# Sending k's rounded parts ahead of q's, and negating the row maxima ahead of k's roundings

## What is computed

```
xn = layernorm(x)
q, k, v = xn Wq + bq, xn Wk + bk, xn Wv + bv      # 32 query heads, 8 key/value heads, width 64
q, k = rope(q) * SCALE, rope(k) * SCALE            # interleaved pairs: first and second component
scores = q . k, masked to |i - j| <= 128, with one sink logit per head
s = softmax([scores, sink])[..., :-1] v, projected by Wo, + bo
g = silu(fp8_quantised(xn) W_ffn + b_ffn)
out = x + s * g
```

## Time and profile before

| what | value |
|---|---|
| runs | 1755.33 us median of 3 (1750.91 to 1756.24) |
| the profiled execution | 1750.54 us, span 1748.8 us |
| mean granted TensorE clock | 0.966 |
| PE busy | 1636.6 us (94% of the span) |
| DVE busy | 1170.5 us (67%) |
| POOL busy | 1024.7 us (59%) |
| ACT busy | 992.4 us (57%) |
| PE waiting at L1126, put down to "issue" | 23.5 us in 8 waits, longest 3.3 us |

### The profile page before, as it was taken

The page is one execution under the profiler, slowest core; times in us unless marked ns, Lnnn a source line. Parts: engine busy times, 40 slices in busy tenths (PEclk is TensorE's granted clock), DMA queues, the critical chain, the costliest instruction groups (busy, mean ns, idle before and its releaser), DMA issues.

```text
span 1748.8 us, 33908 instructions
## 1 busy us (share of the span) xinstructions
PE 1636.6 (94%) x11139; PEld 1466.8 (84%) x11139; DVE 1170.5 (67%) x3643; ACT 992.4 (57%) x2405; POOL 1024.7 (59%) x1019
## 2 busy tenths in 40 slices
PE   3289999999999999999999999999999999999998
PEld 2168998989979898899979999898988999799987
DVE  7766666666767667576666666666775767676664
ACT  2245665666655665556655666556665566555663
POOL 3445656576556656566665755656574676566651
PEclk9579999999999999999999999999999999999999
DMA  4534542535344543454434344355434444434540
GB/s 163 138 64 82 103 79 61 110 70 97 70 86 90 98 91 63 86 94 91 89 69 94 76 95 82 67 103 99 84 61 100 82 94 84 77 69 86 104 82 13
DMA packets 79678, 150.88 MB, mean 86 GB/s; under 512 B 12688, under 2 KB 28816, under 8 KB 75408
## 3 DMA queue, kind: packets, MB, share of 16 engines
q1 hardware_dynamic: 79504, 148.71, 42.6%
HBM read 18.64 MB, written 4.19 MB: 13 GB/s over the span
## 4 chain that ended last, share of the span: by engine, by line
PE 88%; issue 3%; DVE 3%; ACT 1%; POOL 0%; DMA 0%; SPq 0%; POOLq 0%; DVEq 0%
PE pv_bank L1165 29%; PE ring L1071 12%; PE ring L1126 11%; PE acc L1190 10%; PE score L1149 8%; PE score L1151 8%; PE ring L1175 4%; PE ring L1080 3%; PE ring L1102 1%; PE ring L1061 1%; DVE junk L878 1%; DVE ffn_e L773 0%; PE ring L1041 0%; DMA x_in<-in_x 0%; DVE k_first_hi L856 0%
## 5 line engine op out<-in xcount | busy, mean ns | idle before, releaser
L878 DVE CUSTOM_DVE_ANT_0 junk<-ring,mask,sink 128x384 bf16<-128x384 f32 (+1 forms) x1024 | 559.5, 549 | 325.8 <-PE ring L1126 309.3
L1165 PEld LDWEIGHTS pv_bank<-v,stage 128*128 128x128 f32 x5120 | 687.6, 192 | 32.6 <-ACT stage L608 11.1
L1165 PE MATMUL pv_bank<-v,stage 128*128 128x65 f32 x5120 | 688.6, 266 | 4.1 <-DVE o_norm L893 3.2
L528 POOL TENSOR_SCALAR_AFFINE_SELECT stage<-stage 128x512 f32<-128x512 f32 x384 | 251.5, 667 | 506.7 <-ACT stage L608 506.0
L608 ACT ACTIVATE stage<-score 128x512 f32<-128x512 f32 x640 | 372.9, 597 | 217.7 <-PE score L1151 209.0
L1126 PE MATMUL ring<-kT_high,qT_full 128*128 128x384 f32 (+1 forms) x1024 | 372.7, 364 | 46.8 <-issue 23.5
L1149 PE MATMUL score<-qT_full,kT_high 128*128 128x512 f32 x640 | 266.1, 416 | 0.0
L1126 PEld LDWEIGHTS ring<-kT_high,qT_full 128*128 128x128 f32 x1024 | 197.2, 193 | 81.5 <-issue 36.5
L1151 PE MATMUL score<-qT_high,kT_low 68*128 68x512 f32 x640 | 256.0, 400 | 0.0
L666 ACT ACTIVATE oT_hi<-ring 128x256 fp32r<-128x256 f32 x256 | 96.8, 378 | 181.8 <-PE ring L1175 179.9
L643 ACT ACTIVATE qT_high<-ring,ident 4x256 fp32r<-4x256 f32 x512 | 196.0, 451 | 4.7 <-PE ring L1102 1.7
(11 more groups left out here) (114 smaller groups left out, 2605.1 us busy)
## 6 DMA issues: line engine op xcount, KB each, us to landing
qT_high<-qT_full SPq DMA_DIRECT2D x64, 512.0 KB, 4.5
qT_full<-q_first SPq DMA_DIRECT2D x64, 256.0 KB, 4.2
qT_full<-q_first_hi SPq DMA_DIRECT2D x64, 256.0 KB, 5.3
qT_full<-q_second SPq DMA_DIRECT2D x64, 256.0 KB, 4.1
qT_full<-q_second_hi SPq DMA_DIRECT2D x64, 256.0 KB, 5.3
kT_high<-k_first_hi SPq DMA_DIRECT2D x128, 64.0 KB, 2.5
kT_high<-k_second_hi SPq DMA_DIRECT2D x128, 64.0 KB, 2.4
x_res<-in_x SPq DMA_DIRECT2D x11, 512.0 KB, 6.1
```

Source lines behind the costliest of these rows:

```text
L528: nc.gpsimd.affine_select(out=pr, in_=pr, compare_op=ALU.is_ge, fill=0.0, base=0, pattern=[[0, GROUP], [sign, P]], channel_multiplier=-sign) \
L878: nc.vector.tensor_tensor_reduce(junk[:, h % 2, 0:cols], ring[h % 2][:, 0:cols], mask[:, m0:m0 + cols], 1.0, sink[:, col:col + 1], ALU.add ...
L1165: last = nc.tensor.matmul(pv[:, h, :], prob[:, q % 2 * 3 + n, h * P:(h + 1) * P], v[:, slot, k, :], start=(n == 0), stop=(n == len(BLOCKS[ ...
```

## The change

On SP `keys_in` is split. The four transfers of the rounded parts (`keys_high_in`) wait for k's roundings (`s_k_hi`) alone, the two of the low parts (`keys_low_in`) for the subtractions (`s_k_lo`), as before. At k = 6 the four stand in front of the first component of q, and the two stay where all six were. On ACT `negated` moves in front of `keys_first_high`, `chunk_high`, `ffn_exp` and `scale_x`, and `keys_second_high` goes right behind `keys_first_high`.

```
-            def keys_in(t):
+            def keys_high_in(t):
                 quad, r = t // QUAD, slice(t % QUAD, P, QUAD)
-                sp.wait_ge(s_k_lo, 2 * quad + 2)
+                sp.wait_ge(s_k_hi, 2 * quad + 2)
                 upto(sp, s_score_pe, NB * (t - 2))
                 upto(sp, s_kT_in, K_IN * t)
                 for row, part in ((0, k_first_hi), (HALF, k_second_hi), (D, k_first_hi), (D + HALF, k_second_hi)):
                     sp.dma_start(kT_high[row:row + HALF, t % 3, :].bitcast(F32), part[r, :]).then_inc(s_kT_in, 16)
+
+            def keys_low_in(t):
+
+                quad, r = t // QUAD, slice(t % QUAD, P, QUAD)
+                sp.wait_ge(s_k_lo, 2 * quad + 2)
                 for row, part in ((0, k_first), (HALF, k_second)):
                     sp.dma_start(kT_low[row:row + HALF, t % 3, :].bitcast(F32), part[r, :]).then_inc(s_kT_in, 16)
...
                 if real(t) and t % QUAD:
-                    keys_in(t)
+                    keys_high_in(t)
+                    keys_low_in(t)
                 if real(t) and k == 2:
-                    keys_in(t)
+                    keys_high_in(t)
+                    keys_low_in(t)
+                if real(t) and k == 6:
+                    keys_high_in(t)
                 if real(a):
                     queries_in(a, False)
                 if real(t) and k == 6:
-                    keys_in(t)
+                    keys_low_in(t)
                 if real(a):
                     queries_in(a, True)
...
                     if q == 2 and real(a):
                         first_high(a)
+                    if q == 0 and real(it):
+                        negated(it, 1)
+                    if q == 2 and real(b):
+                        negated(b, 0)
                     if (k, q) in ((2, 0), (6, 2)) and quad < BATCH * QUADS:
                         keys_first_high(quad)
+                        keys_second_high(quad)
                     if it < 0 and fill + FIRST_CHUNKS < N_CHUNKS:
                         chunk_high(fill + FIRST_CHUNKS)
                     if (k, q) in ((2, 2), (4, 2)) and 0 <= n < BATCH:
                         ffn_exp(n, k // 2 - 1)
                     if (k, q) == (6, 0) and 1 <= n + 1 < BATCH:
                         scale_x(n + 1)
-                    if q == 0 and real(it):
-                        negated(it, 1)
-                    if q == 2 and real(b):
-                        negated(b, 0)
-                    if (k, q) in ((2, 0), (6, 2)) and quad < BATCH * QUADS:
-                        keys_second_high(quad)
```

## The result

| | before | changed |
|---|---|---|
| median of 4 runs | 1753.12 us (1745.76 to 1756.24) | 1729.70 us (1726.83 to 1737.31) |
| the profiled execution | 1750.54 us | 1731.17 us |
| span | 1748.8 us | 1729.4 us |
| mean granted clock | 0.966 | 0.973 |

The ratio is 0.9882, 95% interval 0.9849 to 0.9916: 1.2% faster. The forecast was 1730.0 us, 25.3 us less than a median of 1755.33; a fourth execution of the kernel before, 1745.76 us, has brought that median down to 1753.12. The medians differ by 23.4 us, the two profiled executions by 19.4 us. What follows explains the 19.4, since the traces are of these.

A forecast was written before the change was run, and what follows sets the result against it. PE, busy for 94%, bounds the kernel, with waits for q's second component at k = 6. 14.9 (queue) + 12.2 (clock) + 2.4 (start-up) - 4.2 (k = 2) = 25.3 us, from 1755.3 to 1730.0 us; range 1722 to 1746.

The forecast's parts named there:

- SP's queue at k = 6: At k = 6, q's second component goes out earlier, so PE restarts 2.13 us earlier a batch, 14.9 us over seven.
- POOL 0.39 us later at k = 6 through `scale_x`: In slot 0 of k = 6, `scale_x` behind `negated` makes the exponentials 0.67 us later; 0.39 us of it remain on POOL.
- PE's arrival: At k = 6, PE was taken to reach its wait at 288.92 as before, leaving a wait of 0.94 us.
- The clock: Behind the waits at k = 6, the shorter wait no longer brings the clock down: 12.2 us, bounds nothing to 14.5.
- k = 2: At k = 2, ACT's roundings behind `negated` delay `max_rows` and PE by 0.53 us, eight times: 4.2 us lost.
- Rival 1: At k = 6, the shorter wait still brings the clock down: 1742 us, chance 0.22.
- The start-up: At the start, q's second component goes out earlier and PE's 9.1 us wait shrinks by 2.4 us, bounds 1 to 2.4.
- Rival 2: At k = 6, q's second component lands later behind its first: only 0.7 us a batch won, about 1752 us, chance 0.05.
- The sum: Over the whole kernel, all terms together gain 25.3 us: profiled execution 1725.2 us, median 1730.0 us.

The follow-up runs named there:

- e1: SP's part of the change alone, ACT's order as in the kernel before: 1713.29 us, ratio 0.9804.
- e2: ACT's part of the change alone, on the kernel before, SP's order as before: 1759.39 us, ratio 1.0060.
- e6: The full change, but with `scale_x` in front of `negated` again in slot 0 of k = 6: 1718.55 us, ratio 0.9823.
- e7: The full change, but with k's first rounding in front of `negated` again in slot 0 of k = 2: 1725.22 us, ratio 0.9853.
- e4: The full change, with k's low parts behind `second_low` on POOL and behind q's second component on SP at k = 6: 1722.44 us, ratio 0.9853.
- e3: SP's part, and of ACT's part only `negated` in front of k's roundings in slot 2: 1716.37 us, ratio 0.9820.
- e5: SP's part alone, with k's low parts last on POOL and SP at k = 6 as in e4: 1710.31 us, ratio 0.9774.
- e8: The kernel of e1 run again, on another chip: 1717.96 us, ratio 0.9810.

## Why the prediction was right, point by point

- **SP's queue at k = 6.** Right. The step that ends at the restart is 2.05 us shorter in batch 0, for the 2.13 forecast. Over the seven batches it is 2.05, 2.1, 2.05 (without the fall in batch 2), 2.1, 1.7, 2.0 and 1.4: 13.5 us for 14.9. The two smallest are batches 4 and 6, where q's second component landed later. e1 shows that the gain needs nothing of ACT's part, e2 that ACT's part has none of its own.
- **POOL 0.39 us later at k = 6 through `scale_x`.** Right: the exponentials began at 262.70 + 1.43 = 264.13 (264.11 worked out), `second_low` ended 0.46 us later against PE (20.66 us behind L1134, where it was 20.20), and e6, without this, has waits of 0.6 us.
- **PE's arrival.** The step that said nothing else changes for PE at k = 6 failed. PE arrived 0.8 us early, so its wait is 1.84 us and more. That costs nothing at the restart but it matters for the clock, below. The cause is on DVE. Two of its operations stand in front of `oT_lo` there, and the first took 1.14 us before and 0.42 after:

```profile
273.49 1.14 DVE L773 TENSOR_SCALAR ffn_e<-x_in 128x512 uint32<-128x512 uint32 x1
```

```profile
272.08 0.42 DVE L781 TENSOR_SCALAR ffn_e<-x_in 128x512 uint32<-128x512 uint32 x1
...
677.77 1.57 DVE L781 TENSOR_SCALAR ffn_e<-x_in 128x512 uint32<-128x512 uint32 x1
```

  POOL's rows beside the three (before; the changed kernel in batches 0 and 2):

```profile
273.07 1.27 POOL L501 TENSOR_TENSOR k_second<-k_second,k_second_hi 128x512 f32<-128x512 f32 x1
```

```profile
272.13 1.52 POOL L510 TENSOR_TENSOR k_second<-k_second,k_second_hi 128x512 f32<-128x512 f32 x1
...
677.77 1.28 POOL L510 TENSOR_TENSOR k_second<-k_second,k_second_hi 128x512 f32<-128x512 f32 x1
```

  Before, DVE started 0.42 us into POOL's operation and ended 0.29 us after it. With POOL 0.47 us later against it, DVE starts 0.05 us ahead and takes 0.42 us, and it is POOL's operation that is longer (1.52). In batch 2 both start at 677.77 and DVE has to wait: 1.57 us. The changed kernel has 0.42 in six batches and 1.57 in one, and e7 has the same. The two others with `negated` first in slot 0 at k = 6, e2 and e4, have 0.42 in all seven. e1, e3, e5, e6 and e8, which keep the old order there, have 1.11 to 1.14 in all seven, as before. So the shift that e6 undoes is the cause. The Trainium skill, SBUF — State Buffer (Who interferes with whom), states that a DVE instruction in a mode that uses two ports and a GpSimd instruction contend for a shared pair of ports, which whoever issues first holds for its whole instruction. The lengths agree with it. That this DVE instruction runs in such a mode, and that the two block each other there, is read from the lengths; it wasn't tried by itself.
- **The clock.** The term that was mis-sized. 12.2 us were taken. Measured: the seven steps behind the restarts sum to 203.58 us before and 196.33 after, 7.2 us less, of which the fall in batch 2 takes back 29.02 - 26.70 = 2.3, so 4.9 us of the 12.2. In the last batch no fall stands behind its wait of 1.33 us, where the earlier trace rows had 0.50. The run behind the last restart at k = 6 is 222.92 - 220.58 = 2.3 us shorter, with the 0.5 us of k = 2 in it, which makes 2.8 us of this. The forecast counted no fall there, and it comes and goes by chance: e1 and e8 are one kernel, and in the 6 us behind the last batch's wait (1.35 and 1.48 us) the one has the full clock and the other has not:

```profile
1670.64:1676.64 6.00, 5.97 (x41) 1.00 0.41 87
```

```profile
1669.56:1675.56 6.00, 6.00 (x32) 0.65 0.41 87
```

  At k = 6 the reason is the arrival above: waits of 1.84 to 2.66 us kept the clock's falls in four batches. With waits of 0.7 us or less, in e1, e3, e5, e6 and e8, all 35 steps behind the restarts are of 27.16 to 27.22 us, so without a fall. The price of a fall was forecast at 1.4 us (0.42 x 3.4) and is 1.6. The Trainium skill, TensorE: Matmul & The Clock Gate (Terms), puts the penalty at the throttled time times (1 - K/N), by which an estimate for 3.4 us is 1.7. The trace nearly agrees, with its 1.6. Rival 1 had this mechanism and 1742 us; it came true in part.
- **The start-up.** Right in kind: 1.8 us less of wait for 2.4 forecast, within its bounds of 1 to 2.4.
- **k = 2.** Right: 0.51 us in batch 0 (the changed kernel is 1.91 us ahead at L1134 in front of it, 1.40 behind it), 0.48 by e6 against e1, for 0.53 forecast.
- **Rival 2, late landings.** In the changed kernel only in part: 6.15 us from the last issue in batch 6 and 5.63 in batch 4, and 5.31 to 5.46 in the others. It appeared in e4, once two components of q stood in front of k's low parts.
- **The sum** for the profiled executions: 13.5 + 4.9 + 2.8 + 1.8 - 8 x 0.51 = 18.9 us, measured 19.4; 0.5 us are not assigned. Forecast were 25.3, so the sum was 5.9 us too high, and 2.8 us of what was measured are the last batch's, which was not in it. That the changed kernel's median came out at the forecast, 1729.70 for 1730.0, is in good part luck: it is 1.5 us below its profiled execution, and the 1755.33 us from which the forecast was taken are 4.8 above the one of before.

## What to carry to other kernels

An idle engine's slot is worth what stands in it: k's first rounding ran while ACT waited for the maxima, and moving the awaited operation to the front turned work that had been free into 0.5 us of path. When a change has two parts, time them apart: here SP's part alone was worth 2.0% and ACT's took it down to 1.2%. A shorter wait may still bring TensorE's clock down, so a forecast has to work out when the engine arrives as well as when it is released.

## What the runs showed of the hardware beside that

- TensorE's clock fell to 1.2 GHz behind waits of 1.24 us (last batch of e2, mean clock 0.65 over the next 6 us), 1.36 (last batch of e6, 0.62), 1.47 and 1.91, and behind two of 0.79 and 0.33 us within a microsecond. It did not fall behind one of 1.42 (last batch of e5) or two of 1.84, nor in e7 behind one of 2.33. How long the wait is does not settle it. Behind the waits at k = 6 of up to 0.71 us it fell in none of the 35 steps.
- A 64 KB transfer of k's low parts landed 2.1 to 2.3 us after its issue in the changed kernel and took 4.8 to 5.1 us right behind q's second component in the same queue (e4).
- Where the spread between runs of one kernel comes from is not shown, but two places of the profiled executions differ. One is the last batch, as above. The other is the start-up: from head 1's first matmul of the maxima to head 2's the profiled executions of e1 and e8, 1719.66 and 1721.26 us, take 37.0 and 37.1 us at a mean clock of 0.68, and that of e3 takes 31.9 us at 0.92. Three of e1's five runs are at 1713, and none of these has a trace.
